# Cross-attention with LoRA on one core: softmax reciprocals that ride in the maximum's tile and are spread by a transfer in SBUF, with the lists of three engines reordered

## The reference

```
lin(x, W, A, B) = x @ W + 2 * (x @ A @ B)
q = lin(x, Wq, Aq, Bq)            # 32 heads of 32
k = lin(ctx, Wk, Ak, Bk)          # 8 heads of 32, each used by 4 query heads
v = lin(ctx, Wv, Av, Bv)
attn = softmax(q k^T / sqrt(32))  # over the 256 rows of ctx
out = x + lin(attn v, Wo, Ao, Bo)
```

## Time and profile before

| | |
|---|---|
| time, median of 3 runs | 734.06 us (733.98 to 735.76) |
| the profiled execution's own time | 734.93 us |
| its span, first to last instruction | 733.1 us |
| TensorE matmul busy | 715.6 us (98%) |
| VectorE busy | 465.7 us (64%) |
| ScalarE busy | 446.6 us (61%) |
| GpSimd busy | 246.4 us (34%) |
| mean granted TensorE clock | 0.990 |

### The profile page before, as it was taken

One profiled execution on the slowest core, in us unless ns is written; L12 is line 12 of the kernel. 1 busy time (PEld: TensorE's weight loads), 2 busy tenths in 40 slices (PEclk: granted clock), 3 DMA queues, 4 the chain that ended last, 5 costly groups with the idle time before them and its releaser, 6 DMA issues.

```text
span 733.1 us, 15768 instructions
## 1 busy us (share of the span) xinstructions
PE 715.6 (98%) x5248; PEld 611.6 (83%) x5248; DVE 465.7 (64%) x833; ACT 446.6 (61%) x1418; POOL 246.4 (34%) x246
## 2 busy tenths in 40 slices
PE   6989999999999999999999999999989999999998
PEld 6768888888888888888888888888757788888886
DVE  4947877787777777678678778778876321222211
ACT  3547788788878878878788878788976211011100
POOL 3662731550641245165134406505456300000000
PEclk8999999999999999999999999999989999999999
DMA  6777663465356346435735733654674533454231
GB/s 234 268 226 191 186 178 120 123 195 174 109 179 199 124 152 188 142 98 176 202 109 157 200 122 115 196 175 137 188 228 138 187 129 113 161 172 138 91 114 57
DMA packets 94785, 117.10 MB, mean 160 GB/s; under 512 B 8736, under 2 KB 76320, under 8 KB 94752
## 3 DMA queue, kind: packets, MB, share of 16 engines
q1 hardware_dynamic: 94752, 116.69, 51.0%
HBM read 78.91 MB, written 37.75 MB: 159 GB/s over the span
## 4 chain that ended last, share of the span: by engine, by line
PE 89%; DVE 4%; ACT 3%; DMA 2%; issue 1%; POOL 1%; SPq 0%; DVEq 0%
PE banks L1043 34%; PE banks L1116 23%; PE banks L1061 9%; PE banks L1105 9%; PE banks L1086 8%; PE banks L1096 2%; PE banks L1077 2%; ACT banks L706 1%; PE banks L1028 1%; DMA probs_t<-b4kv 1%; DVE w_sum L827 1%; PE banks L1030 1%; DVE neg_max L857 1%; POOL k_stack L583 1%; DMA probs_t<-wq 1%
## 5 line engine op out<-in xcount | busy, mean ns | idle before, releaser
L706 ACT ACTIVATE banks<-banks,neg_max 128x256 f32<-128x256 f32 x512 | 229.2, 449 | 63.5 <-DVE neg_max L857 63.5
L857 DVE TENSOR_REDUCE neg_max<-banks 128x2 f32<-128x512 f32 x256 | 175.7, 687 | 53.0 <-PE banks L1061 51.0
L717 ACT ACTIVATE probs_t<-banks 128x512 f32<-128x512 f32 x256 | 154.3, 603 | 44.8 <-PE banks L1086 44.3
L1043 PE MATMUL banks<-x_hi,w_hi 128*128 128x256 f32 x512 | 144.8, 283 | 1.2 <-DVE q_stage L850 0.7
L1043 PE MATMUL banks<-x_lo,w_hi 128*128 128x256 f32 x512 | 144.8, 283 | 0.0
L1043 PE MATMUL banks<-x_hi,w_lo 128*128 128x256 f32 x512 | 144.6, 282 | 0.0
L633 POOL TENSOR_TENSOR rsum_cols<-rsums,ones 128x256 f32<-128x256 f32 x64 | 39.5, 618 | 220.4 <-PE banks L1096 220.2
L1061 PE MATMUL banks<-k_stack,q_stack 96*128 96x256 f32 x512 | 110.1, 296 | 1.6 <-ACT banks L706 1.2
L1086 PE MATMUL banks<-q_stack,k_stack 104*128 104x512 f32 x256 | 107.9, 421 | 0.0
L706 ACT ACTIVATION_READ_ACCUMULATOR banks<-banks,neg_max 128x1 f32 x512 | 104.8, 205 | 0.0
L1061 PEld LDWEIGHTS banks<-k_stack,q_stack 96*128 96x128 f32 x512 | 79.7, 190 | 29.1 <-ACT banks L706 14.7
(11 more groups left out here) (109 smaller groups left out, 1393.4 us busy)
## 6 DMA issues: line engine op xcount, KB each, us to landing
q_stack<-q_parts SPq DMA_DIRECT2D x192, 128.0 KB, 2.6
q_parts<-q_stage SPq DMA_DIRECT2D x64, 256.0 KB, 2.2
raw<-ct SPq DMA_DIRECT2D x32, 256.0 KB, 5.1
raw<-xt SPq DMA_DIRECT2D x32, 256.0 KB, 4.4
context<-ctx_stage SPq DMA_DIRECT2D x64, 128.0 KB, 2.1
stage<-xn SPq DMA_DIRECT2D x16, 512.0 KB, 4.2
w_hi<-context SPq DMA_DIRECT2D x14, 512.0 KB, 6.0
out<-raw SPq DMA_DIRECT2D x13, 512.0 KB, 2.9
```

What stands on the lines that cost most here:

```text
L706: last = nc.scalar.activation(score_bank[c % 2][:, S * h:S * (h + 1)], score_bank[c % 2][:, S * h:S * (h + 1)], ACT.Exp, bias=neg_max[:, u ...
L717: nc.scalar.activation(probs_t[:, u % 2, t, 2 * hp:2 * hp + 2, :].rearrange("p a b -> p (a b)"), st_bank[j % 2], ACT.Exp, scale=-1.0).then ...
L857: nc.vector.tensor_reduce(out=neg_max[:, u % 2, 2 * c:2 * c + 2], in_=score_bank[c % 2].rearrange("p (h t) -> p h t", h=2), axis=AXIS, op= ...
L1043: mm = nc.tensor.matmul(proj_bank[bank][:, 0:S], lhs, rhs, start=(k == 0), stop=(k == GROUP_MM - 1))
```

## The change

The columns 0 to 3 of both halves of `max_parts`, unused so far, take the reciprocals of the unit (`reciprocal` now writes there, after that unit's maximum was turned). The next unit's turn of the maximum turns them along. VectorE copies the whole turned tile from PSUM to `turned_sb` (`copy_turned`, c = `TURN` = 2). From there GpSimd places the maximum, two heads at a time (`place_max`, 8x512 each), and a DMA on SP's queue (`spread`) reads rows 0 to 3 and writes each 32 times, to the 128 partitions of `scales`. `widen`, the two transposes before the context products, and the copy of the scales from PSUM are gone; `normalize` waits for the DMA and moves from c = 1 to c = 3. The last unit needs one more turn.

The lists change too. GpSimd's input splits stand in slots 3, 7, 8 and 11 instead of 3, 4, 6 and 7; for the next x it makes the high parts only, and VectorE makes the four remainders in slots 15, 17, 18 and 19 (`LOW_SLOTS`). ScalarE makes the projections' high parts ahead of the exponentials of the slot. SP loads inputs in four places instead of together. In the last batch `fold_mms` comes first in TensorE's slot, `w_high` in the same slot as `fold_mms`, `w_low` in the next, the fold slots 8, 9, 12, 13 become 9, 10, 13, 14, and SP's loads of the output weights are spread out.

```diff
+TURN = 2
+SPLIT_SLOTS = ((3, 7, 8, 11), (3, 4, 7, 8))
+LOW_SLOTS = (15, 17, 18, 19)
+FIRST_SPLIT = (28, 31, 32, 33)
-FOLD_SLOTS = (8, 9, 12, 13) + tuple(range(16, 28))
+FOLD_SLOTS = (9, 10, 13, 14) + tuple(range(16, 28))
-        scale_rows = banks[:, 5, 0:S]
-        max_rows = banks[0:KM, 5, S:2 * S]
+        turned = banks[0:KM, 5, 0:S]
 # SP
+                def spread(g):
+                    wait(turned_out, unit0 + (g + 2))
+                    need(sp, ctx_done, unit0 + (g - 1))
+                    sp.dma_start(scales[:, g % 2], turned_sb[0:GH, (g + 1) % 2].unsqueeze(1).broadcast_to([GH, HD, S])
+                                 ).then_inc(r_spread[g % 2], DMA)
...
+                load_x(2)
+                spread(1)
                 store_ctx(0)
...
 # GpSimd
+            def place_max(b, u, hp):
+                rows, heads = slice(3 * HD, KM), slice(2 * hp, 2 * hp + 2)
+                if hp == 0:
+                    pool.wait_ge(turned_out, b * NG + (u + 1))
+                nc.gpsimd.tensor_tensor(q_stack[rows, u % RING, heads],
+                                        turned_sb[rows, u % 2].unsqueeze(1).broadcast_to([M_ROWS, 2, S]),
+                                        head_mask[rows, heads].unsqueeze(2).broadcast_to([M_ROWS, 2, S]),
+                                        ALU.mult).then_inc(max_placed, 1)
+                pool.wait_ge(max_placed, b * (2 * NG) + (2 * u + hp + 1))
...
-                if c == 1 and not (first and u < 1):
-                    widen(b, u - 1)
+                if last:
+                    for f in fold_chunks(s - 1):
+                        w_low(f)
+                        pool.wait_ge(w_lo_pool, sums_to(f))
+                if c == TURN and u >= 0 and not (last and u >= NG):
+                    for hp in range(2):
+                        place_max(b, u, hp)
 # ScalarE
                     exp_turned(b, u - 1, c)
+                if not last and (s > FIRST or s == FIRST and not first):
+                    proj_highs(b, s, last)
                 if s + AHEAD > 0 and not (last and s + AHEAD - 1 >= SLOTS):
                     exps(b, s + AHEAD - 1)
...
-                if not last:
-                    proj_highs(b, s, last)
-                    for f in fold_chunks(s - 1):
+                    for f in fold_chunks(s):
                         w_high(f)
 # VectorE
+            def reciprocal(b, u):
+                dve.wait_ge(exp_done, b * SLOTS + (4 * u + 4))
                 dve.wait_ge(max_turned, b * NG + (u + 1))
+                nc.vector.reciprocal(max_parts[:, :, 0:GH],
+                                     sums[:, u % 2, :].rearrange("p (a h) -> p a h", a=2)).then_inc(rsum_done, 1)
+            def copy_turned(b, u):
+                dve.wait_ge(max_turned, b * NG + (u + 1))
+                need(dve, max_placed, b * (2 * NG) + 2 * (u - 1))
+                need(dve, r_spread[(u + 1) % 2], b * (4 * DMA) + DMA * ((u - 3) // 2 + 2))
+                nc.vector.tensor_copy(turned_sb[:, u % 2, :], turned).then_inc(turned_out, 1)
             def normalize(b, u):
-                dve.wait_ge(rsum_turned, b * NG + (u + 1))
-                need(dve, ctx_done, b * NG + u)
-                nc.vector.tensor_copy(scales[:], scale_rows).then_inc(scales_done, 1)
-                dve.wait_ge(scales_done, b * NG + (u + 1))
+                dve.wait_ge(r_spread[u % 2], b * (4 * DMA) + DMA * (u // 2 + 2))
...
-                if c == 1 and not (first and u < 2):
-                    normalize(b, u - 2)
-                if c == 2 and here:
-                    place_max(b, u)
+                if c == TURN and u >= 0 and not (last and u > NG):
+                    copy_turned(b, u)
                 if c == 3 and here:
                     reciprocal(b, u)
+                if c == 3 and not (first and u < 2):
+                    normalize(b, u - 2)
 # TensorE
-                if j == 0:
-                    pe.wait_ge(max_placed, b * NG + (u + 1))
+                if j < 2:
+                    pe.wait_ge(max_placed, b * (2 * NG) + (2 * u + j + 1))
...
-                pe.wait_ge(rsum_wide, b * NG + (u + 1))
-                for qh in range(2):
-                    last = nc.tensor.transpose(
-                        scale_rows[:, P * qh:P * (qh + 1)],
-                        rsum_cols[:, GH * qh:GH * (qh + 1), :].rearrange("p h d -> p (h d)"), ident[:])
-                last.then_inc(rsum_turned, 1)
```

More of the change, by code:

```diff
@@ L429, in body @@
                 stack_q(4, fills + 3, st0 + 4)
+                load_x(1)
                 send(pos["q", 5, 0])
+                load_x(2)
+                spread(1)
                 store_ctx(0)
-                for j in range(4):
-                    wait(c_ready, b * 4 + (j + 5))
-                    load_inputs(xt, b + 1, j)
                 send(pos["q", 6, 0])
                 stack_q(5, fills + 3, st0 + 8)
+                load_x(3)
+                spread(2)
                 send(pos["q", 7, 0])
+                load_context(b + 2, 0)
@@ L455, in body, with load_context @@
                 stack_q(2, fills + 6, st0 + 28)
-                store_ctx(6)
-            def load_context(b):
-                for j in range(4):
+                spread(7)
+            def load_context(b, *chunks):
+                for j in chunks:
                     wait(x_ready, (b - 1) * 4 + (j + 1))
@@ L506, in last_body @@
                     load_rows(0, h)
+                first_loads(0, 1)
+                spread(0)
+                store_ctx(-1)
+                send(4)
+                first_loads(2)
+                stack_q(4, fills + 3, st0 + 4)
+                late_loads(4)
+                first_loads(3)
+                spread(1)
+                late_loads(5)
+                store_ctx(0)
+                send(5)
+                late_loads(6)
+                stack_q(5, fills + 3, st0 + 8)
+                late_loads(7)
+                spread(2)
+                store_ctx(1)
+                send(6)
+                late_loads(8)
+                stack_q(6, fills + 4, st0 + 12)
+                late_loads(9)
+                spread(3)
+                late_loads(10)
+                store_ctx(2)
+                send(7)
+                late_loads(11, 12)
+                stack_q(7, fills + 4, st0 + 16)
+                late_loads(13)
+                spread(4)
+                late_loads(14)
                 store_ctx(3)
-                late_loads(13, 14)
+                late_loads(15)
                 for i in range(2):
@@ L966, in slot @@
                         w_total(f)
-                else:
-                    proj_lows(b, s, last)
+                proj_lows(b, s, last)
+                if not last:
+                    if s in LOW_SLOTS:
+                        j = LOW_SLOTS.index(s)
+                        input_low(x_hl, j, x_hi_done, x_ready, b * 4 + (j + 5))
             for s in range(-AHEAD, FIRST + SLOTS):
@@ L974, in _ @@
                     slot(b, s, False, False)
-            for s in range(FIRST, SLOTS + 6):
+            for s in range(FIRST, SLOTS + 8):
                 slot(NB - 1, s, False, True)
@@ L1151, in slot @@
                 u, c = divmod(s, 4)
-                if c == 2 and u >= 0 and not (last and u >= NG):
-                    turn_max(b, u)
+                if last:
+                    for f in fold_chunks(s):
+                        if f == FOLD_O:
+                            stack_ready(pe, 2)
+                        if f in (FOLD_O, FOLD_O + 2, FOLD_O + 4):
+                            pe.wait_ge(proj_out, b * PER + (PRO + 1 + (f - FOLD_O) // 2))
+                        fold_mms(f)
+                if c == TURN and u >= 0 and not (last and u > NG):
+                    turn_max(b, u, last and u >= NG)
                 if not (first and u < 1) and not (last and u > NG):
```

147 lines of the change are left out of this document (63 added, 84 removed).

## The result

| | before | changed | e1: changed, 16 source rows |
|---|---|---|---|
| time, median | 734.02 us | 802.27 us | 720.23 us |
| ratio to before, 95% interval | | 1.0919 (1.0871 to 1.0968) | 0.9821 (0.9805 to 0.9838) |
| span of the profiled execution | 733.1 us | 800.8 us | 717.4 us |
| mean granted TensorE clock | 0.990 | 0.966 | 0.997 |
| a middle batch | 62.80 us | 70.84 us | 60.89 us |

The change makes the kernel 9% slower; 719.1 was forecast, in a range of 711 to 729. The third column takes the cause ahead: where the new transfer reads sixteen rows instead of four, and the reciprocals are written to as many columns, the time is near the forecast's.

A forecast was written before the change was run, and what follows sets the result against it. TensorE's own instructions were taken to bound seven of eight batches. From 734.93 us, 13.4 for the pairs, 0.5 for the first batch and 1.0 for the last gave 720.0, by the median 719.1 us; range 711 to 729.

The forecast's parts named there:

- The spread crowds the queues: Rival on the DMA queues: late weight loads in the last batch cost 5 us in all, 725.2 us; chance 0.10.
- Cost nothing: Verdict on the new transfer per unit: landing in 2.6 us, at most 6.0, under 8.3 us of cover.
- SP and the spread: Step on SP's list with one more 128 KB transfer per unit, 64 in all, claimed to cost nothing.
- my signs: Prediction wrong if a transposed product waits for GpSimd, normalization waits for a transfer, or the weight-sum wait grows.
- 8.3 us of cover: Time from the copy's end, 1.3 us after a turn, to the normalization needing the spread, 9.6 us after it.
- The pair: Two TensorE transposes of widened reciprocals removed per unit: 0.21 us each, 64 pairs, 13.4 us saved, ends 9.0 and 19.8.
- The placement: GpSimd's half placement ahead of the transposed score product: 1.04 to 1.30 us per piece, no wait counted.
- the move: Four input remainders per batch from GpSimd to VectorE, 0.68 us each, 1.64 at worst; claimed to cost nothing.
- The first batch: TensorE's 0.75 us wait for VectorE's q remainder, with 0.8 us less VectorE work ahead: -0.5 us.
- The last batch: Lighter VectorE against GpSimd's added weight remainders and placements, near balance: -1.0 us, ends -5.6 and +5.
- The sum: Whole kernel: 734.93 - 13.4 - 0.5 - 1.0 = 720.0 us, by the median 719.1.
- one rival alone, the placement: Placement misses its deadline at each unit's first transposed product: 752.6 us, or 804 at 3.20 us per piece; chance 0.12.

The follow-up runs named there:

- e5: The changed kernel with 8 source rows for the spread instead of 4, each written 16 times: 723.33 us, ratio 0.9863 to before.
- e6: The changed kernel with its four-row spread split into four transfers, one per row: 776.33 us, ratio 1.0605 to before.
- e8: The changed kernel with 16 source rows, ScalarE's high parts of the projections behind the exponentials again except in the last batch: 730.28 us.
- e9: The changed kernel with 16 source rows, high part and remainder of the next x back on GpSimd in slots 14 to 17: 762.02 us.
- e11: The changed kernel with its four-row spread moved behind the next q stacking in SP's list, except in the last batch: 884.40 us.

## Why the prediction was wrong

**The step that failed** is the rival *The spread crowds the queues*, and with it "Cost nothing" in *SP and the spread*. It put the four-row transfer at 2.0 us on each of four queues, without a wait in the body and with at most 5 us in the last batch. The runs showed 10 us in each middle batch and 82 us in all (802.27 against 720.23 in e1). The mechanism was named, and four queues was right. Four things were wrong:

- I weighed the queues by their mean load: "At four, these engines go from 52% to ... 78% in the body, no wait". A mean says nothing on a burst. The 33 packets of each of four queues stand in front of whatever is issued next, once per unit, and the q store and the context's store land 4.9 and 5.0 us later. The room of the q chain was counted for the stacking alone ("about four slots ... for the 2.6 us it takes to land"), but the chain is store, wait of SP for its landing, stacking: 2.2 + 2.6 before, 7.1 + 2.9 = 10.0 us after, against 7.85 for a unit; in e5 it is 4.6 + 3.0 = 7.6, and the middle batches lose nothing. SP's list was taken as free, and it is nearly full: 60.4 us of issues in a batch of 70.84, with the waits for landings besides. No run tells the share of the landings in the loss from that of the list.
- The spread's own landing was put at 2.6 us, at most 6.0. With four rows it is 7.0 us and more (issue at 321.74, normalization at 328.77), and SP issues it late besides (SP waits for the turned tile only 8.0 us in all, in 3 waits, against 89.2 us in 36 in e1: it comes to the spread when the tile has long been there). One of my signs came true by that: the normalization waits for a transfer, 29.2 us in all, with 8.3 us of cover on paper. So did the others: TensorE's wait for the weight sum is 6.1 us against 2.6 before, and its transposed products wait 2.7 us in all for GpSimd, which is little. With sixteen rows the spread lands in 3.5 us, and neither the normalization nor TensorE's product for the weight sum waits.
- I priced the packet at 63 ns, the mean of all; the spread's took, by the estimate of e6, 14 us / 132 = 106 ns. So 3.5 us per queue, not 2.0. The landings grew by 4.9 us; the other 1.4 are not accounted for.
- I put the damage into the last batch and bounded it by 5 us in all. It was 10 us and more in each batch (70.84 against e1's 60.89; 71.5 to 72.3 in the four batches beside it). Of the 10, 7.6 are idle time of TensorE, and in 63.24 - 60.89 = 2.4 the same products take longer. The granted clock of that batch, 0.98 (1.00 in e1), gives 0.02 x 70.84 = 1.4 of the 2.4 by estimate; the rest is open. Over the whole kernel TensorE's busy time is 723.9 us with the four rows and 698.2 in e1, with 5122 matmuls in both; there the clocks, 0.966 and 0.997, give 0.034 x 800.8 - 0.003 x 717.4 = 25 of the 25.7 us.

**The rest of the sum** can be read in e1, which differs only in the rows and the columns that hold them:

- The pair: predicted 0.21 us; (62.80 - 60.89) / 8 = 0.24. The slot with the context products, from transposed product to transposed product, went from 304.12 - 301.16 = 2.96 to 304.93 - 302.19 = 2.74 us. Right, and 2 us too small in the sum. TensorE's timeline of e1:

```profile
302.19 0.40 PE L1142 MATMUL banks<-q_stack,k_stack 104*128 104x512 f32 x1
303.59 1.07 PE L1155 MATMUL banks<-probs_t,v_sb 128*32 128x256 f32 x16
304.59 0.50 PE L1115 MATMUL banks<-k_stack,q_stack 96*128 96x256 f32 x2
304.93 0.40 PE L1142 MATMUL banks<-q_stack,k_stack 104*128 104x512 f32 x1
```

- The placement: 1.04 to 1.30 us taken, 1.06 measured, in the changed kernel and e1. No wait of TensorE for it in the middle batches of e1: right, and e8 shows a part of what it rested on.

```profile
L682 POOL TENSOR_TENSOR q_stack<-turned_sb,head_mask 8x512 fp32r<-8x512 f32 x128 | 135.9, 1062 | 197.8 <-DVE turned_sb L937 192.1
```

- VectorE: 41.0 us per batch expected, 40.13 in e1. The remainders took 0.683 at the median and 1.845 at most; they hid. I costed the move at nothing, which held in the direction taken. That it was needed (e9) I had not seen.

```profile
L949 DVE TENSOR_TENSOR x_lo<-raw,x_hi x32: 678/683/1845, 27.3 to 462.4; 128x512 fp32r<-128x512 f32 x32
```

- The first batch: -0.5 taken. Its term is not there: at the turn of the maximum that starts at 109.44 before and at 108.61 in e1, five pairs are gone (1.2 us), and e1 is 0.8 ahead, so about +0.4.
- The last batch: -1.0 taken. Its first turn of the maximum starts at 501.91 before and 489.12 in e1; from there to the end are 733.1 - 501.91 = 231.2 us and 717.4 - 489.12 = 228.3. The nine pairs that are left and the one new turn explain 1.9 of the 2.9, so about -1.0: right, but as the balance of two larger things. TensorE waits 1.61 and 1.46 us for the placement in e1, once behind the move of V and once behind input splits and a weight remainder, as I feared, and twice 0.7 us for ScalarE. On the other side it waited 1.64 and 0.52 us for the weight sum before and then ran at half clock, where e1's clock stays at 1.00.

```profile
500.06 0.50 PE L1142 MATMUL banks<-q_stack,k_stack 104*128 104x512 f32 x1 [1.61 <-POOL q_stack L682]
508.66 0.50 PE L1142 MATMUL banks<-q_stack,k_stack 104*128 104x512 f32 x1 [1.46 <-POOL q_stack L682]
```

- The sum: 719.1 predicted, 720.23 in e1. That they are so near is in part luck: the pairs gave 2 us more and the first batch 0.9 less than taken, and the two profiled spans differ by 733.1 - 717.4 = 15.7 us, the medians by 13.8.

The chance of slower, 0.12, was held for one rival alone, the placement. The four queues stood in the text, and I let them change only the price of the smallest stage.

## What to carry to other kernels

A transfer is to be judged by the queues it uses and by what stands behind it, not by the mean load: count the outermost rows of both sides, take its packets per queue, and add that time to the landing of each transfer that is issued next, along its whole chain of store, wait and load. Sum the issues of the queue's list too: a list that is full delays everything in it. A broadcast from a few partitions can be given sixteen rows almost for nothing where the producer can write its values several times (here 342 ns for a reciprocal instead of 192). And an engine with half of its time free (GpSimd is busy for 45% in e9) can still miss a deadline: look at the longest run of instructions ahead of the one that is awaited.

## What the runs showed of the hardware that was not expected

- Four source rows against sixteen, same bytes: 829.97 against 735.68 us in the kernel before, where no engine reads what the transfer writes.
- The transfer of four rows lands 7.0 us and more behind its issue (321.74 to 328.77), the one of sixteen rows in a median of 3.5 us.
- Four one-row transfers of sixteen queues each: by estimate from the shares 45 us of engine time for 128 KB, against 14 with four or sixteen rows in one transfer and 9 with sixty-four.
- A DMA issue on SP's list two places behind the four-row transfer took 2.83 us, where the same line takes 0.34 us undisturbed (e11), so such a transfer also holds the list behind it: 60.4 us of issues in a batch, against 27.6 with sixteen rows.
- An 8x512 product on GpSimd takes 1.06 us, as long as the 128x512 one (1.04): fewer partitions make it no shorter.
